# Gated delta heads: how the projection weights are loaded and turned

## The reference, cut to what matters

```
q = silu(causal_conv(x @ Wq.T))     # conv over 4 tokens, per channel
k = silu(causal_conv(x @ Wk.T))
v = silu(causal_conv(x @ Wv.T))
q, k = l2norm(q), l2norm(k)
# per token: S = g*S + outer(k, beta*(v - g*(S.T @ k)));  o = S.T @ q
o = rmsnorm(o) * norm_w * silu(x @ Wg.T)
return o @ Wo.T
```

## Time and profile before

| | us |
|---|---|
| median of 3 runs | 3418.72 (3413.23 to 3420.4) |
| profiled execution, its own time | 3415.16 |
| its span | 3413.4 |
| first matmul of `delta_heads` (turn of head 0) | 82.40 |
| first matmul of the loop over heads | 130.20 |
| first DMA of the part after `delta_heads` | 1715.70 |

### The profile page before, as it was taken

The page is one execution under the profiler, slowest core; times in us unless marked ns, Lnnn a source line. Parts: engine busy times, 40 slices in busy tenths (PEclk is TensorE's granted clock), DMA queues, the critical chain, the costliest instruction groups (busy, mean ns, idle before and its releaser), DMA issues. The chain is left out here.

```text
span 3413.4 us, 60026 instructions
## 1 busy us (share of the span) xinstructions
PE 3180.1 (93%) x18834; PEld 2544.9 (75%) x18834; DVE 2191.9 (64%) x4849; ACT 1898.9 (56%) x4657; POOL 1672.6 (49%) x3107
## 2 busy tenths in 40 slices
PE   6899999999999999999999788799979999998998
PEld 3688888888888888888878555488866777776543
DVE  5577777777777777777653488765547567574432
ACT  3677777777777777777532377644445445363111
POOL 2777787777788777778630000145534002011322
PEclk9899999999999999999999999999989999999999
DMA  4222222222222222222353333423351222211854
GB/s 113 63 73 69 59 69 62 73 68 67 74 55 73 62 73 68 65 76 53 97 176 92 115 142 142 177 87 103 115 174 57 68 69 69 93 65 53 271 99 56
DMA packets 432408, 310.47 MB, mean 91 GB/s; under 512 B 130496, under 2 KB 347456, under 8 KB 431072
## 3 DMA queue, kind: packets, MB, share of 16 engines
q1 hardware_dynamic: 423792, 289.57, 28.8%
q0 software_dynamic: 8432, 18.88, 2.8%
HBM read 177.97 MB, written 130.43 MB: 90 GB/s over the span
## 5 line engine op out<-in xcount | busy, mean ns | idle before, releaser
L631 PE MATMUL gd_PJ<-xn_lead,gd_w_rest 128*128 128x512 f32 x1024 | 421.3, 411 | 0.5 <-DVE gd_w_rest L786 0.5
L631 PE MATMUL gd_PJ<-xn_lead,gd_w_lead 128*128 128x512 f32 x1024 | 403.0, 394 | 0.0
L631 PE MATMUL gd_PJ<-xn_rest,gd_w_lead 128*128 128x512 f32 x1024 | 401.9, 393 | 0.0
L1079 POOL TENSOR_TENSOR gd_prod<-gd_L,gd_T 32x14 f32<-32x14 f32 (+6 forms) x896 | 324.8, 362 | 70.4
L1082 POOL TENSOR_TENSOR gd_T<-gd_T,gd_prod 32x14 f32<-32x14 f32 (+6 forms) x896 | 311.6, 348 | 71.6 <-POOL gd_prod L1079 2.5
L793 DVE SCALAR_TENSOR_TENSOR gd_conv<-gd_pre,gd_cur_a,gd_conv 128x512 f32<-128x512 f32 x384 | 301.8, 786 | 13.3 <-ACT gd_conv L958 2.9
L631 PEld LDWEIGHTS gd_PJ<-xn_lead,gd_w_lead 128*128 128x128 f32 x1024 | 193.8, 189 | 43.4
L631 PEld LDWEIGHTS gd_PJ<-xn_lead,gd_w_rest 128*128 128x128 f32 x1024 | 194.4, 190 | 38.5 <-DVE gd_w_rest L786 0.9
L631 PEld LDWEIGHTS gd_PJ<-xn_rest,gd_w_lead 128*128 128x128 f32 x1024 | 194.6, 190 | 35.3
L932 DVE SCALAR_TENSOR_TENSOR gd_og<-gd_B,ptab,gd_gate 128x512 f32<-128x512 f32 x64 | 48.1, 751 | 243.8 <-PE gd_B L645 243.8
L2619 ACT ACTIVATE sa_E<-sa_B,sa_nmax 128x512 f32<-128x512 f32 (+3 forms) x256 | 131.3, 525 | 131.4 <-DVE sa_nmax L2756 127.2
(11 more groups left out here) (476 smaller groups left out, 8620.3 us busy)
## 6 DMA issues: line engine op xcount, KB each, us to landing
expert_rows<-xt_blank SPq DMA_DIRECT2D x16, 2112.0 KB, 7.3
turned_queries_keys<-f_wq SPq DMA_DIRECT2D x16, 1280.0 KB, 6.0
x_wo<-decay_sums SPq DMA_DIRECT2D x64, 256.0 KB, 3.7
triangles<-gd_Lo SPq DMA_DIRECT2D x64, 256.0 KB, 3.5
gd_W<-turned_image SPq DMA_DIRECT2D x64, 256.0 KB
gd_T<-inverse_image SPq DMA_DIRECT2D x64, 256.0 KB
gated_outputs<-gd_og SPq DMA_DIRECT2D x64, 256.0 KB, 2.8
go_ogt<-gated_outputs SPq DMA_DIRECT2D x16, 1024.0 KB, 5.9
```

The lines of the kernel that those rows point to most:

```text
L631: mm = pe.matmul(bank, w_parts[wp][:, j, k, :], rhs, start=(k == 0 and wp == 1), stop=(k == KT - 1 and wp + xp == 0))
L1079: nc.gpsimd.tensor_tensor(prod[:, rows, 0:j], L16[:, rows, j:j + 1].to_broadcast(shape), T16[:, j:j + 1, 0:j].to_broadcast(shape), ALU.mul ...
```

## The change

Each weight slice is loaded in 16 DMAs of 32 rows by 4 x 32 columns (`load_blocks`). Block (r, c) of each 128x128 tile goes to block (c, r) of `wraw`, so that turning each 32x32 block by itself turns the whole tile. VectorE does that with one instruction per slice into a new SBUF buffer `wT` (two halves, Wk and Wq share one, Wv and Wg the other); `w_lead` and `w_rest` are made from `wT` instead of from PSUM. TensorE's turns and their waits are gone. Head 0's 64 pieces are loaded in `front`; of head 1, 48 pieces (Wk, Wv, Wq) are loaded before SyncE's slot -2; in the loop each slot loads one slice, 16 pieces, between the row of decay sums and the spread. VectorE turns Wk in c=0, Wv in c=1, Wq and Wg in c=2, each ahead of the gated output (line 932), and the parts are made in the same places as before (c=1, c=2, c=3). The buffers `R` and `osqr` are dropped: line 849 writes `Vb` in place, the squares of line 1014 go back to their PSUM bank and those of line 1036 to `oi`.

```diff
+SIDE32 = 32
+W_LOADS = 16 * (P // SIDE32) ** 2
+def load_blocks(sp, wraw, j, src, done):
+    n = P // SIDE32
+    for c in range(n):
+        for r in range(n):
+            dst = wraw[c * SIDE32:(c + 1) * SIDE32, j, :].rearrange("p (k r x) -> p k r x", k=KT, r=n)[:, :, r]
+            rows = src[r * SIDE32:(r + 1) * SIDE32, :].rearrange("p (k c x) -> p k c x", k=KT, c=n)[:, :, c]
+            sp.dma_start(dst, rows).then_inc(done, 16)
...
 # front, SyncE
-                sp.dma_start(wraw[:, j, :], A[n][0:P, :]).then_inc(w_in, 16)
+                load_blocks(sp, wraw, j, A[n][0:P, :], w_in)
...
 # delta_heads, SyncE
-            def load_weights(h):
-                for j, n in enumerate(W_NAMES):
-                    sp.dma_start(wraw[:, j, :], A[n][bass.ds(h * P, P), :]).then_inc(w_in, 16)
+            def load_weights(h, j):
+                sp.wait_ge(w_turned, h * 4 - 4 + j + 1)
+                load_blocks(sp, wraw, j, A[W_NAMES[j]][bass.ds(h * P, P), :], w_in[j])
...
-            def slot(i, c, back, has1, has2, more):
+            def slot(i, c, back, has1, has2, more, fetch=False):
                 n = i * CH + c
                 if more:
                     load_row(i, c)
+                if fetch:
+                    load_weights(i + 1 if c == 0 else i + 2, (JG, JK, JV, JQ)[c])
                 if has1:
                     spread(n + 1, (c + 1) % 2)
...
             sp.wait_ge(w_turned, 4)
-            load_weights(1)
+            for j in (JK, JV, JQ):
+                load_weights(1, j)
...
             with sp.Fori(0, HEADS - 2) as i:
                 for c in range(CH):
-                    slot(i, c, True, True, True, True)
-                sp.wait_ge(w_turned, i * 4 + 8)
-                load_weights(i + 2)
+                    slot(i, c, True, True, True, True, True)
...
 # TensorE: turn_weights and its calls removed; one wait before project(JV) and project(JK)
...
 # VectorE
-                nc.vector.tensor_tensor(rest, PJ[:, W_BANK[j], :], lead.bitcast(F32), ALU.subtract).then_inc(w_copied, 1)
+                nc.vector.tensor_tensor(rest, wT[:, W_SIDE[j], :], lead.bitcast(F32), ALU.subtract).then_inc(w_copied, 1)
+            def turn_weights(h, j, held):
+                dve.wait_ge(w_in[j], h * W_LOADS + W_LOADS)
+                if held is not None:
+                    dve.wait_ge(w_copied, held)
+                nc.vector.transpose(wT[:, W_SIDE[j], :], wraw[:, j, :]).then_inc(w_turned, 1)
...
+                if back and more:
+                    for j in ((JK,), (JV,), (JQ, JG), ())[c]:
+                        turn_weights(i + 1, j, i * 4 + 3 + j)
...
+            turn_weights(0, JK, None)
             rest_weights(0, JK, 0)
+            turn_weights(0, JQ, 1)
+            turn_weights(0, JG, None)
...
+            turn_weights(0, JV, 3)
...
 # ScalarE
-                nc.scalar.copy(w_parts[0][:, j].rearrange("p k n -> p (k n)"), PJ[:, W_BANK[j], :]).then_inc(w_lead, 1)
+                nc.scalar.copy(w_parts[0][:, j].rearrange("p k n -> p (k n)"), wT[:, W_SIDE[j], :]).then_inc(w_lead, 1)
...
             lead_weights(0, JK, 0)
             lead_weights(0, JQ, 1)
+            lead_weights(0, JG, 2)
             act.wait_ge(head_k, 1)
             act.wait_ge(k_proj, 1)
             copy_pre(0, PK, JK, cur_k, k_pre)
-            lead_weights(0, JG, 2)
             lead_weights(0, JV, 3)
```

More of the change, by code:

```diff
@@ L171, in _ @@
             sp.dma_start(rows_dram.rearrange("h c b t -> (h c b) t").rearrange("(g p) t -> p g t", p=P), rows[:, :, :]).then_inc(rows_out, 16)
[L172 removed]
+            sp.wait_ge(w_in, W_LOADS * 4)
             sp.wait_ge(rows_out, 16)
@@ L439, in delta_heads @@
         w_parts = [sb(n, [P, 4, KT, P], F32R) for n in ("w_lead", "w_rest")]
+        wT = sb("wT", [P, 2, DIM])
         cur_k = sb("cur_k", [P, PW])
@@ L488, in delta_heads @@
         half = [Bk[k][:, 0:2, :].rearrange("p a (h c) -> p (a h) c", h=2) for k in range(6)]
-        cst_in, w_in, image_in, wo_in = sem("cst_in"), sem("w_in"), sem("image_in"), sem("wo_in")
+        cst_in, image_in, wo_in = sem("cst_in"), sem("image_in"), sem("wo_in")
+        w_in = [sem(f"w_in{j}") for j in range(len(W_NAMES))]
         og_out = [sem("og_out0"), sem("og_out1")]
@@ L513, in delta_heads @@
         W_BANK = (0, 0, 1, 1)
+        W_SIDE = (0, 1, 0, 1)
         PK, PQ, PV = 0, 1, 2
@@ L582, in _ @@
                 sp.dma_start(cst[:, j * P:(j + 1) * P], const_dram[:, col:col + P]).then_inc(cst_in, 16)
-            sp.sem_inc(w_in, 64)
+            for j in range(len(W_NAMES)):
+                sp.sem_inc(w_in[j], W_LOADS)
             sp.wait_ge(zeroed, 1)
@@ L611, in _ @@
                         sp.dma_start(wo[:, j, :], A["Wo"][j * P:(j + 1) * P, :]).then_inc(wo_in, 16)
-                    slot(i, c, True, i < LAST or c < CH - 1, i < LAST or c < CH - 2, i < LAST)
+                    slot(i, c, True, i < LAST or c < CH - 1, i < LAST or c < CH - 2, i < LAST, i < LAST and c == 0)
             sp.wait_ge(wo_in, 16 * KT)
@@ L618, in _ @@
         def _(pe):
-            def turn_weights(h, j):
-                pe.wait_ge(w_in, h * 64 + 64)
-                for k in range(KT):
-                    tr = pe.transpose(PJ[:, W_BANK[j], k * P:(k + 1) * P], wraw[:, j, k * P:(k + 1) * P], ident)
-                tr.then_inc(w_turned, 1)
             def project(j, cm, done):
@@ L678, in merge @@
                         each(half[3][0:TOP], [T_c[:, b, 0:TOP] for b in range(B)], [Y[:, l % 2, b, :] for b in range(B)], wup)
-                if back and more and c == CH - 1:
-                    pe.wait_ge(g_silu, n + 2)
-                    turn_weights(h1, JQ)
                 if back:
@@ L695, in slot @@
                     project(JQ, c1, q_proj)
-                if back and more and c == 1:
-                    pe.wait_ge(k_pre, n + 3)
-                    turn_weights(i + 1, JK)
                 if back:
@@ L711, in slot @@
                     spread_rows(2)
-                if back and more and c == CH - 1:
-                    pe.wait_ge(q_pre, n + 2)
-                    turn_weights(h1, JG)
                 if has1:
@@ L719, in slot @@
                         pe.wait_ge(v_pre, n + 3)
-                    if back and more and c == 1:
-                        pe.wait_ge(w_copied, (i + 1) * 4 + JK + 1)
-                    else:
-                        pe.wait_ge(w_copied, h1 * 4 + JV + 1)
+                    pe.wait_ge(w_copied, h1 * 4 + JV + 1)
                     project(JV, c1, v_proj)
@@ L738, in slot @@
                         pe.wait_ge(s_ready, n + 1)
-                    each(Bk[1], tiles(W_c), tiles(R if c > 0 else Vb), u_sum)
+                    each(Bk[1], tiles(W_c), tiles(Vb), u_sum)
                 if has1:
@@ L748, in slot @@
                     each(Bk[1], tiles(Kd), tiles(U), s_sum)
-                if back and more and c == 2:
-                    pe.wait_ge(v_pre, n + 4)
-                    turn_weights(i + 1, JV)
                 if has1:
@@ L848, in slot @@
                     for b in range(B):
-                        st = nc.vector.scalar_tensor_tensor(out=R[:, b, :], in0=Bk[1][:, b, :], scalar=twice[:, par, 1, b:b + 1],
+                        st = nc.vector.scalar_tensor_tensor(out=Vb[:, b, :], in0=Bk[1][:, b, :], scalar=twice[:, par, 1, b:b + 1],
                                                             in1=Vb[:, b, :], op0=ALU.mult, op1=ALU.add)
```

14 lines of the change are left out of this document (2 added, 12 removed).

## The result

The changed kernel takes 3453.31 us (median of 4 runs, 3447.01 to 3460.83), the kernel before 3419.56 (median of the 4 runs beside them, 3413.23 to 3421.26). The ratio is 1.0111, with a 95% interval of 1.0097 to 1.0126: **slower by 34 us**, where 15 us less had been forecast. It lies above the range, and the sign is the other one. It is the fastest of the four.

What follows compares the result with a forecast made beforehand. The prediction took TensorE to bound the loop, the solve chain second. Removing its turns gave -26 us, the later start +11.1, in sum -14.9 from 3415.16: 3400.3, or 3404 as median; range 3389 to 3424 for 8 in 10.

Steps and rivals of the forecast that it cites:

- The slack of the solve chain: Loop: GpSimd's 3.50 us wait in c=3 keeps 1.8 us after TensorE's head shortens by 1.7; chain cost taken as nothing.
- Rival B: Loop: the solve chain becomes the bound, growing 2.7 us a head, 0.9 too much, 14 us in all: 3418; chance 0.18.
- The rest from two SBUF inputs: Rival B's mechanism: four rests a head, each blocking GpSimd's solve for 0.68 us, so the chain grows by 2.7 us.
- The spacing of SyncE's issues: SyncE, front, start and loop: 0.49 us per piece, bounds 0.36 and 0.58; a slot's 16 make 7.8 us.
- The front's cover: SyncE in front: 64 pieces hidden before the row sums' store at 77.36, 5.9 us to spare; costs above 0.58 spacing.
- the start: SyncE before the loop: 48 pieces delay the row load and the first solve by 11.1 us; bounds +4.9 and +15.4.
- C: SyncE, front and start: pieces issue slower than slices; front costs 64s - 36.8, start 48s - 12.4; 3433 at 0.8; chance 0.14.
- TensorE's turns: Loop: removing four turns a head saves 1.73 us, 26 us over 15 heads; bounds 16 and 37 us.
- The turn of quarter 1: TensorE in c=1: one of the head's four removed turns, forecast to save 0.44 us.
- VectorE's 64 turns: Ahead of the gated output: 0.699 us each, 2.8 us a head, hidden in idle time, so nothing; 42 us without cover.
- Pieces in the loop: SyncE, between row and spread: 16 DMAs a slot, 7.8 us in a 12.4 us gap, cost nothing up to 0.78 spacing.
- The signs named for B: Loop: the solve chain as bound would show as TensorE's DMA waits in more than one slot a head.

Runs made afterwards that it cites:

- e13: e4 with SyncE storing the next triangle ahead of the wait for the spread's landing; 41.6 us below e4, 0.7% faster than the kernel before.
- e3: Kernel before, turns still on TensorE, only the rest taken from two SBUF inputs (identity in place of the PSUM bank, values wrong): 3429.15 us, ratio 1.0035.
- e10: Kernel before with the last 3 of the solve's 14 elimination steps left out (inverse incomplete): 3394.70 us, ratio 0.9935.
- e9: e4 with the last 3 of the solve's 14 elimination steps left out (inverse incomplete): 3368.01 us, ratio 0.9855.
- e1: Changed kernel with the slices of heads 0 and 1 loaded ahead of the loop whole, one DMA each; pieces in the loop: 3432.78 us, ratio 1.0046.
- e2: Changed kernel with every slice loaded whole by one DMA, in the loop too (blocks in wrong order): 3431.74 us, ratio 1.0044.
- e4: Changed kernel with four DMAs a slice in 512-byte runs instead of sixteen, same product: 3433.64 us, ratio 1.0050.
- e5: e2 with the rest written as zeros by a memset that reads no input: 3425.64 us, ratio 1.0027.
- e6: e4 with GpSimd's copy of the next head's constants moved ahead of its wait for the triangle's blocks; 8 us between e4 and this run.
- e8: e6 with the rest parts as zeros by a memset, left out of the product; 16 us above the 3392 to 3400 expected.

## Why the prediction was wrong

**The slack of the solve chain: the step that turned the sign.** The forecast took TensorE's list as the bound of the whole head and its shortening as the gain, "as long as nothing else is next", and put what the chain might take at nothing. That is the step that failed. Rival B allowed the chain 1.8 us more a head, because GpSimd's only wait for the others was 3.50 us at 1023.20 and 1.7 of it would go. The mean times between the chain's stations, over heads 2 to 13, are these (spread to triangle store, to fetch, to the start of the solve, to its second half, to the next spread):

```
              spread-store  store-fetch  fetch-start  start-second  second-spread   all
before  c=0       3.23         3.54         5.46          1.25          15.17      28.66
        c=1       3.33         3.48         2.09          0.92          13.59      23.41
        c=2       3.24         3.49         2.06          1.11          14.02      23.91
        c=3       3.24         3.60         2.09          1.11          13.72      23.75
after   c=0       3.26         3.66         4.52          1.26          15.09      27.78
        c=1       3.33         3.45         1.96          1.04          15.01      24.79
        c=2       3.25         3.42         1.98          1.11          14.03      23.78
        c=3       3.26         3.51         2.14          1.11          14.10      24.12
```

(c is here the slot in whose solution the chain goes around, counted from the one with GpSimd's jump.) Three things go against the forecast here.

*The chain held the head in half of it already.* From the fetch to the start it takes 2.0 to 2.1 us in every slot but c=0, before and after, which is the landing of the fetch: GpSimd starts the moment the blocks are there. (In e13 the same step takes 3.4 us and more in each slot, so there the blocks lie ready.) What lengthens the chain in these three slots isn't caught by a wait of GpSimd somewhere else in the head: in e3 the rests made the head 0.94 us longer while GpSimd still waited 3.25 us a head at the place of the 3.50. And with the chain short (e10) quarters 1 and 2 of the kernel before take 24.84 and 24.82 us, where they took 25.81 and 25.30. So 1.5 us of the head of 99.73 were the chain's, and the rest TensorE's. The view of the waits had it before: GpSimd waited for the triangle's blocks 44 times in 60 slots (the second line of the fence of before above), and I had read only TensorE's side of that view, with its 14 slots.

*The slack was real, but smaller than read.* Behind the 3.50 us GpSimd goes through its jump and its row and begins the solve without waiting for the blocks:

```profile
1027.32 0.20 POOL L1098 TENSOR_TENSOR gd_tiny<-gd_none 128x4 f32<-128x4 f32 x1 [2.69 <-issue]
...
1031.05 1.17 POOL L1069 TENSOR_TENSOR gd_T<-gd_L,gd_below 32x256 f32<-32x256 f32 x1
```

Over heads 2 to 13 that wait is 3.49 us on the mean, and the blocks have landed 3.5 us before the solve starts. In the changed kernel 0.74 of it stays, about as much as the wait of 0.72 in the slot after, which both kernels have. So 2.75 us could be used up, 1.0 beyond the 1.7 forecast for TensorE and not 1.8.

*The chain grew more than charged.* A head less this wait is 96.24 us before (99.73 - 3.49) and 99.74 after (100.48 - 0.74), 3.5 us longer where B charged 2.7. Some 1.7 of it lie in the second half of the solves of c=1 and c=3 (the table), 1.7 in GpSimd's own work between two solves at the jump, 0.5 in the wait at the jump. With 3.5 in place of 2.7 and 1.0 in place of 1.8, B's sum gives 2.5 us a head on top of the forecast 98.00, the head that was measured.

Seen from TensorE: the head of before is 1.48 us above e10's (98.25), that of the changed kernel 3.56 above e9's (96.92; e9 has four DMAs a slice). The 2.1 more are 31 us over 15 heads, the turns gave 20, and 11 is left, for 10.0 in the trace.

**The rest from two SBUF inputs: right in kind, one of the causes.** B's mechanism was named, with 2.7 us a head on GpSimd. Measured, GpSimd is 45 us busier over 15 heads, 3.0 a head. From 200 to 1700 us 7 us of it lie on line 1100 (58 times 1158 - 1036 ns), 27 in the small steps of the solve, where lines 1079 and 1082 rose by 16 and 17 ns, 840 times each, and 14 on line 1125 (60 times 635 - 400 ns). B's price was too low all the same: it charged 0.9 us a head, and the head grew to 100.48 from a forecast 98.00, 2.5 us, 37 us over 15 heads. e3 puts 12 us to the two inputs alone.

**The spacing of SyncE's issues: mis-sized.** 0.49 us was taken from slices of 128 partitions and 2 KB runs. A piece of 32 partitions with 128-byte runs needs 0.64, outside my bounds of 0.36 and 0.58. The front's cover of 0.58 was passed by that, 4.1 us, and the start cost 19.4 and not 11.1. C's two formulas, 64s - 36.8 and 48s - 12.4, give 4.2 and 18.3 at 0.64, 22.5 together, and the first solve is 22.7 us late; of these the shorter first solve gave 3.2 back, which the forecast didn't have, so that C's term of the start, 18.3, meets the 19.4 by luck. e1, e2 and e4 show that the issues are the whole of it. No row of before had a DMA of that shape, and durations of 0.31 to 0.48 over three other shapes don't say what sets them; the bound should have reached farther up, as rival C's did.

**What held.** TensorE's turns in quarters 2 and 3: 1.29 us a head by start-to-start times, 1.29 between e10 and e9, with quarter 3 at 24.36 for a forecast of 24.2 (24.67 in the changed kernel). The turn of quarter 1 was mis-sized, 0.44 forecast and 0.04 measured, so a head gives 1.33 and not 1.73. VectorE's 64 turns, 0.70 us each, cost nothing in its idle time:

```profile
L779 DVE STREAM_TRANSPOSE gd_wT<-x_wo x64: 662/696/712, 86.0 to 1630.0; 128x512 f32<-128x512 f32 x64
```

Pieces in the loop cost nothing (e1 and e2), since 10.7 us of issues, begun at 1005.73, end well before the spread of 1020.83. The signs named for B were TensorE's DMA waits in more than one slot a head; they stayed at 14 slots (13.4 us), and the delay came in through VectorE's W instead, 8.5 us in 16 slots before and 24.8 in 43 after. That sign would have misled.

**What stays open**: how much of GpSimd's 45 us comes from the rests and how much from taps that fall elsewhere in its solve (e3 has 17.3 from the rests in the kernel before, e5 takes 20.9 away); why the first solve is shorter; and why GpSimd's wait at the jump grew from 2.6 to 3.1 us a head.

## What to carry to other kernels

Follow a chain that runs through several engines once around, station by station, and count the slots in which each hand-over takes only the landing time. Where that is nearly every slot, the loop has two bounds: what is removed from one gives little, and what lengthens the other there is paid at once, even if an engine of the chain waits for the others at one place of the round. Such a wait is slack only at its own place, and only down to what stays of it in any case (0.7 of 3.5 us here). Before work is moved to an engine that shares SBUF reads with the chain's engine, shorten the chain; a store queued behind a landing that it doesn't need is the cheapest place. A DMA's issue time is to be taken from one of the same shape, and the start of the loop, where nothing covers it, is where many small ones are paid.

## What the runs showed of the hardware that was not expected

SyncE needed 0.564 us (0.64 from start to start) to issue a DMA of 32 partitions with 128-byte runs and 16 KB, more than for a slice of 256 KB in as many runs of 2 KB (0.38, 0.49 from start to start), and 0.47 from start to start for 64 KB in 512-byte runs at the start of the heads; the landing took 2.0 us in the median for the pieces, one beside the other. (The 2 us of fixed cost that the prediction takes from the Trainium skill, "DMA: Bandwidth & Descriptors", stand there under Anatomy of one DMA — SWDGE (gpsimd) path, in a fit for DMAs issued by GpSimd, and not under Rules for kernel authors; these were SyncE's.)

A VectorE operation of 0.68 us with two SBUF inputs made a GpSimd one of 128x512 take 1.50 us in place of 1.04, 15 times of 15; as a memset (0.49 us, no input) or with one input from PSUM it left it at 1.04.

GpSimd waits 2.7 to 3.5 us at the jump back of its loop, once a head, with nothing that releases it. It was 26.7 us over 10 heads before (10.1 more over the other 4, where the view names an operation of ScalarE) and 44.1 over 14 after, and 3.8 over 14, never above 0.3, in both kernels whose loop body is shorter by six instructions a slot (e9, e10). No run was made on its cause; over the heads it sums to more than the 26.7 us of the change.

With the copy of the constants moved ahead and the chain still long (e6 and e8) TensorE's granted clock fell to half, 1.2 GHz, for 3.4 to 6.8 us in four heads of each. In the longest such quarter of e8 (524.11 to 552.28) TensorE had waited 1.37 us for the solved triangle until 526.08, the drop starts at 528, and the quarter takes 28.2 us at a mean clock of 0.88. All eight drops start 1.7 to 2.4 us after such a wait of 1.1 to 1.7 us. The changed kernel had 14 such waits, up to 1.6 us, and kept the full clock, and no run was made on what brings it down.
